# A second PSUM bank for the jobs of a batch, all exponentials of the scan in SBUF, and a new spacing of every job

## The chip, the cores and the metric

The kernel runs on one core of one Trainium2 chip. The metric is the device time in microseconds (us), the median of several executions of the program.

## The reference, cut to what matters

Eight sequences of 512 tokens with 128 channels go through one block: four branches are added to `x`, and then a layer norm and a feed-forward projection follow.

```
xn = layernorm(x) * g + b ;  xp = xn @ w_xproj            # dt_in, B, C (64 states)
delta = softplus(dt_in @ w_dt + b_dt)
h_t = exp(delta_t * A) * h_(t-1) + (delta_t * xn_t) * B_t # 128 channels x 64 states
ssm  = (sum_n h_t * C_t + x * D) @ w_ssm_out
attn = softmax(windowed scores of 16 heads, windows of 32) @ v @ wo
conv = silu(depthwise convolution of x over 4 taps)
mem  = x @ w_wm + 0.3 * softmax(x @ dec.T / sqrt(128)) @ dec   # 512 slots
x1 = x + 0.2 attn + 0.45 ssm + 0.15 conv + 0.2 mem
out = x1 + layernorm(x1) @ W2 + bias                      # W2: int4-rounded weight + low rank
```

## The kernel before, in words

One sequence is a batch, and the kernel's body runs once for each of the 8 batches. The state recurrence sets its beat. It is cut into 64 units. A unit is 2 channels x 64 states on the 128 partitions, 512 steps long, and is one `tensor_tensor_scan` on VectorE. Four units (`q` = 0 to 3) make a group, so a batch has 16 groups. Every engine runs the same loop over the slots `s` = 0 to 63, and what it issues in a slot is written out in its `body`; each engine works in program order and waits on semaphores. Two parities `p` keep the data of one batch apart from those of the next.

What a unit needs:

- ScalarE (`unit_exp`, two slots ahead): the decay `exp(delta * A)` out of `wide`, rows of delta that SyncE's DMA spread over the partitions. For q = 0, 1, 2 it goes to `decay` in SBUF; for q = 3 it goes to the PSUM bank `uP[3]` (line 659).
- The input `delta * xn * B`. For q = 0, 1, 2 TensorE spreads the rows into `uP[q]` (line 905) and VectorE multiplies by `B2` in place (line 1189). For q = 3 the rows come by DMA into `uwide` in SBUF, and GpSimd multiplies them (`pool_input`, line 1407).
- VectorE's scan (line 1201). Of its two inputs one lies in PSUM and one in SBUF, in each of the four cases.
- GpSimd (`pair_product`, line 1391) multiplies the states of two units by C, and TensorE adds them up (`reduce_group`, line 929).

Beside it, in slots of their own, lie the windowed attention of the same batch (scores, line 938; bias and maximum on VectorE, 1214; exponentials on ScalarE, 673; scaling on GpSimd, `prob_norm`, 1396; transposes, 945; values, 953), and the jobs. A job is some matmuls into the PSUM bank `jobP` (bank 7), emptied by ScalarE or VectorE. There are three families, and all share that one bank in the order of `JOB_AT`: "p" prepares the next batch (transposes, dtpre, B, C, q, k, v), "m" is the memory branch (es: scores, pt: transposes of the probabilities) and the convolution of this batch, and "t" ends the batch before (back, zT, ffn). TensorE fills a job only when the job before it in the bank has been emptied (`fill`). ScalarE empties it in the same slot (`EMPTY_LAG` 0). `AT` gives the slots of the other steps: among them `ln_apply`, `scale_xn`, `normalise2`, the softplus chain, `output` (VectorE waits for the ffn job, line 1261), and `gate` (VectorE waits for ScalarE's tanh, line 1236). The projection that gathers the branches (`project`) has 11 steps. In the last batch six of them come before the end of the loop, and the others in `tail`.

Of the kernel before, what the change touches and what calls it, by code (L numbers as in the profile page):

```python
# [12 lines left out]
L = 512  # L13
# [31 lines left out]

JOB_AT = {13: ("t", "back"), 15: ("p", "xaT"), 17: ("p", "xnT"), 19: ("p", "dtpre"),
# [3 lines left out]
EMPTY_LAG = 0  # L50
N_EARLY = 6
JOB_SLOT = {name: s for s, (_, name) in JOB_AT.items()}
# [12 lines left out]
SETUP_AT = 5  # L65


ROWS_AT = {"store": 14, "rows": 15}
VALUE_DMA_AT = {0: (0, 1, 2), 1: (3, 4, 5), 2: (6, 7, 8), 3: (9, 10, 11)}
PART_DMA_AT = {17: 0, 19: 1, 20: 2}  # L70

M_MAX_LAG, M_EXP_LAG, M_INV_LAG, M_DIAG_LAG = 2, 3, 4, 5

SCORES_AT = {33 * k // 10: k for k in range(NBLK)}
BIAS_LAG, EXP_LAG, INV_LAG, NORM_LAG, PT_LAG, PT_COPY_LAG, PV_LAG, AO_COPY_LAG = 2, (3, 4), 6, 5, 9, 9, 11, 11
AHEAD = 2
# [7 lines left out]
def memory_tile_at(s, lag):  # L86

    fam, name = JOB_AT.get(s - lag, ("", ""))
    return int(name[2]) if name[:2] == "es" else None
# [26 lines left out]
def hybrid_block_kernel(nc, x, ln_g, ln_b, w_xproj, w_dt, b_dt, A_log, D_ssm, w_ssm_out, wq, wk, wv,  # L116
# [3 lines left out]
    with ctx:  # L120
# [231 lines left out]
        def _(sp):  # L352
# [142 lines left out]
        def _(act):  # L495
# [132 lines left out]
            def front(B, p):  # L628
# [3 lines left out]
                for name in PRE:  # L632
                    if name == "dtpre":
                        decay_rates()
                    if name == "B":
                        softplus_exp(B)
                        softplus_logs(B)
                    if name == "q":
                        high_parts(B)
                        mid_parts(B)  # L640
                        for part in (1, 2):
                            spread_parts(act, B, p, part)
                        act.wait_ge(const_ready, 3)
                        act.wait_ge(head_tables, 3)
# [48 lines left out]
            def mem_exp(B, t):  # L693
                wait(act, m_max, B * NT + t + 1)
                if t >= 2:
                    wait_job(act, "m", B, f"pt{t - 2}")
                ins = nc.scalar.activation(mprob[:, t % 2, :], jobP[:, :], ACT.Exp, bias=mmx[:, t:t + 1],
                                           accum_out=msum[:, t:t + 1])
# [9 lines left out]
            def memT_copy(B, t):  # L708
                wait_job(act, "m", B, f"pt{t}")
                if t == 0:  # L710
                    wait(act, ready["t"], B * N_TAIL - N_TAIL + 1)
                nc.scalar.activation(mprobT[:, :, t * 128:(t + 1) * 128],
                                     jobP[:, :].rearrange("p (c t) -> p c t", c=4), ACT.Copy).then_inc(done["m"], 1)

            def conv_bias(B):
                wait_job(act, "m", B, "conv")
                wait(act, ready["t"], B * N_TAIL - N_TAIL + 1)
                nc.scalar.activation(cv_v[:, :], jobP[:, :], ACT.Identity, bias=bconv_col).then_inc(cv_step, 1)
                wait(act, cv_step, B * N_CV + CV["v"])
# [26 lines left out]
            def body(B, p):  # L746
                for s in range(UNITS):
# [29 lines left out]
                    if s - EMPTY_LAG in JOB_AT:  # L777
                        empty_job(*JOB_AT[s - EMPTY_LAG], B, p)
                    fam, name = JOB_AT.get(s - 1, ("", ""))
                    if fam == "p" and name in "qk" and not last(B):  # L780
# [27 lines left out]
        def _(pe):  # L808
# [47 lines left out]

            before = [None]

            def fill(fam, B, name):
                if before[0] is not None:  # L860
                    f, b, n = before[0]
                    wait(pe, done[f], job_count(f, b, n))

            def filled(ins, fam, B, name):
                ins.then_inc(ready[fam], 1)
                before[0] = (fam, B, name)

# [89 lines left out]
            def conv_tap(B, p, tap):  # L957
                if tap == 0:
                    fill("m", B, "conv")
                o = HALO - (TAPS - 1) + tap  # L960
                ins = mm(jobP[:, :], convdiag[:, tap, :], xaT[p][:, o:o + L], start=(tap == 0), stop=(tap == TAPS - 1))
                if tap == TAPS - 1:
                    filled(ins, "m", B, "conv")

            def mem_job(name, B, p):
                fill("m", B, name)
                if name[:2] == "es":
                    t = int(name[2])
                    ins = mm(jobP[:, :], xaT[p][:, HALO + t * 128:HALO + (t + 1) * 128], decTs[:, :], start=True,
                             stop=True)  # L970
                else:
                    t = int(name[2])
                    wait(pe, m_diag, B * NT + t + 1)
                    for c in range(4):
                        ins = mm(jobP[:, c * 128:(c + 1) * 128], mprob[:, t % 2, c * 128:(c + 1) * 128],  # L975
                                 mdiag[:, t % 2, :], start=True, stop=True)
# [49 lines left out]
            def body(B, p):  # L1026
                before[0] = ("p", B, "v")
                for s in range(UNITS):
# [30 lines left out]
                    if fam == "p" and not last(B):  # L1059
                        pre_job(name, B + 1, 1 - p)  # L1060
                    if fam == "m" and name != "conv":
                        mem_job(name, B, p)
# [17 lines left out]
        def _(dve):  # L1080
# [391 lines left out]
```

## Time and profile before

| | us |
|---|---|
| median of 3 runs | 1167.07 (1165.49 to 1168.94) |
| profiled execution, its own time | 1166.9 |
| its span, first to last instruction | 1165.1 |
| VectorE (DVE) busy | 988.3 (85%) |
| GpSimd (POOL) busy | 951.5 (82%) |
| TensorE (PE) busy | 866.0 (74%) |
| ScalarE (ACT) busy | 835.1 (72%) |

Busy time is the time in which an engine had at least one instruction under way. Idle time before a group of instructions is put down to what released its first wait. The first scan of batch 0 begins 37.7 us after the start of the span, and the last scan of batch 7 ends at 1141.0 us; the rest is the tail.

### The profile page before, as it was taken

The numbers are of one execution on the slowest core, as the hardware profiler recorded it, in microseconds if no ns is written. First come the engines' busy times: TensorE is split into PE (matmuls) and PEld (weight loads), VectorE is DVE, ScalarE is ACT, GpSimd is POOL, SyncE is SP. The second block draws the span as 40 slices with busy tenths as digits, with TensorE's granted clock in tenths as the row PEclk, the third lists the DMA queues.
The fourth block names the chain that finished last, engine by engine and source line by source line (L and its number), as shares of the span: only waits on it lengthen the run. The fifth ranks groups of instructions, "written<-read, shape, count | busy, mean of one in ns | idle before, by whom it ended". The sixth has DMA issues, their size and how long they took to land. (4 is left out here: it accounts for less than half of the span.)

```text
span 1165.1 us, 19124 instructions
## 1 busy us (share of the span) xinstructions
PE 866.0 (74%) x4151; PEld 361.1 (31%) x4151; DVE 988.3 (85%) x2306; ACT 835.1 (72%) x2247; POOL 951.5 (82%) x668
## 2 busy tenths in 40 slices
PE   4477769687786787777786777867768687778775
PEld 2132323232333233333232333323233233333332
DVE  2699998888897997979989799788998989898992
ACT  4668786877778776777777777587776876766671
POOL 6479997988888887888979898698887988788892
PEclk8558998778897977979889788787989788897797
DMA  5845766565756566566656476555666566656640
GB/s 121 202 127 147 199 164 171 133 169 163 181 153 159 156 158 165 146 155 167 165 166 165 118 192 169 141 147 148 173 167 177 137 166 169 174 157 173 159 113 9
DMA packets 124397, 181.18 MB, mean 156 GB/s; under 512 B 29266, under 2 KB 41062, under 8 KB 124262
## 3 DMA queue, kind: packets, MB, share of 16 engines
q1 hardware_dynamic: 123974, 179.56, 58.9%
q14 instruction: 96, 0.79, 0.3%
q8 instruction: 39, 0.64, 0.2%
q10 hardware_dynamic: 288, 0.20, 0.1%
HBM read 170.79 MB, written 5.05 MB: 151 GB/s over the span
## 5 line engine op out<-in xcount | busy, mean ns | idle before, releaser
L1391 POOL TENSOR_TENSOR prod<-hst,C 128x1024 f32<-128x1024 f32 x256 | 601.7, 2353 | 156.7 <-DVE hst L1201 155.9
L1201 DVE TENSOR_TENSOR_SCAN hst<-decay,bank 128x512 f32<-128x512 f32 x384 | 459.5, 1206 | 16.0 <-POOL prod L1391 15.1
L659 ACT ACTIVATE decay<-wide,A_rep 128x512 f32<-128x512 f32 x384 | 273.9, 715 | 72.8 <-DVE hst L1201 55.0
L1189 DVE TENSOR_TENSOR bank<-bank,B 128x512 f32<-128x512 f32 x384 | 261.7, 681 | 48.8 <-PE bank L938 23.0
L905 PE MATMUL bank<-spread,sel_bc 96*128 96x512 bf16 x384 | 170.0, 444 | 145.3 <-DVE hst L1201 137.0
L673 ACT ACTIVATE prob<-s_sb,nmax 128x96 f32<-128x96 f32 x512 | 184.8, 363 | 1.5 <-DVE nmax L1214 0.5
L1407 POOL TENSOR_TENSOR uwide<-uwide,B 128x512 f32<-128x512 f32 x128 | 162.7, 1271 | 21.8 <-DMA uwide<-u_rows 21.8
L929 PE MATMUL bank<-prod,sel_red 128*32 128x512 f32 x1024 | 171.7, 750 | 2.0 <-POOL prod L1391 2.0
L1201 DVE TENSOR_TENSOR_SCAN hst<-bank,uwide 128x512 f32<-128x512 f32 x128 | 155.0, 1211 | 6.1 <-ACT bank L659 4.6
L938 PE MATMUL bank<-k,q 128*128 128x384 f32 x256 | 133.6, 609 | 7.3 <-DVE nmax L1214 4.8
L945 PE MATMUL bank<-ident,prob 128*96 128x128 f32 x512 | 99.4, 328 | 48.9 <-ACT ao L689 44.2
L905 PEld LDWEIGHTS bank<-spread,sel_bc 96*128 96x128 bf16 x384 | 41.5, 108 | 282.4 <-DVE hst L1201 231.0
L682 ACT ACTIVATE probT<-bank 96x512 f32<-96x512 f32 x128 | 75.1, 587 | 68.4 <-PE bank L945 68.4
L1396 POOL TENSOR_TENSOR prob<-prob,pinv 128x384 f32<-128x384 f32 x128 | 108.9, 851 | 5.7 <-DVE pinv L1222 5.4
L945 PEld LDWEIGHTS bank<-ident,prob 128*96 128x96 f32 x512 | 64.9, 149 | 118.4 <-issue 101.5
L1214 DVE CUSTOM_DVE_ANT_0 s_sb<-bank,bias 128x96 f32<-128x96 f32 x512 | 97.8, 246 | 0.0
L673 ACT ACTIVATION_READ_ACCUMULATOR prob<-s_sb,nmax 128x1 f32 x512 | 96.8, 189 | 0.0
L659 ACT ACTIVATE bank<-wide,A_rep 128x512 f32<-128x512 f32 x128 | 87.0, 680 | 10.8 <-DVE hst L1201 10.8
L689 ACT ACTIVATE ao<-bank 128x128 f32<-128x128 f32 x128 | 33.8, 264 | 64.6 <-PE bank L953 64.6
L938 PEld LDWEIGHTS bank<-k,q 128*128 128x128 f32 x256 | 53.8, 232 | 65.3 <-issue 35.1
L953 PE MATMUL bank<-probT,vw 96*8 96x128 f32 x1024 | 54.2, 285 | 11.2 <-ACT probT L682 11.1
L975 PE MATMUL bank<-mdiag,mprob 128*128 128x128 f32 x256 | 44.0, 326 | 9.5 <-ACT mdiag L706 7.7
(188 smaller groups left out, 1014.6 us busy)
## 6 DMA issues: line engine op xcount, KB each, us to landing
wide<-dt_rows SPq DMA_DIRECT2D x512, 256.0 KB, 4.6
uwide<-u_rows SPq DMA_DIRECT2D x128, 256.0 KB, 4.1
spread<-parts SPq DMA_DIRECT2D x66, 32.0 KB, 3.4
x_sb<-in_L_attn_x_dram SPq DMA_DIRECT2D x8, 256.0 KB, 4.1
dt_rows<-sp_t SPq DMA_DIRECT2D x8, 256.0 KB, 3.9
out_dram<-outb SPq DMA_DIRECT2D x8, 256.0 KB, 2.3
vw<-v_tok SPq DMA_DIRECT2D x80, 16.0 KB, 3.3
u_rows<-uv SPq DMA_DIRECT2D x8, 64.0 KB, 3.6
```

The source lines that it names most:

```text
L659: nc.scalar.activation(to, wide[m % SLOTS][:, s % 2, :], ACT.Exp, scale=A_rep[:, g:g + 1]).then_inc(exp_done, 1)
L673: ins = nc.scalar.activation(prob[:, k % 4, g, :], s_sb[:, k % 2, g, :], ACT.Exp, bias=nmax[:, k % 2, g:g + 1], scale=-1.0, accum_out=psum ...
L905: mm(uP[q][:, :], sel_bc[:, i, :, :].rearrange("k j n -> k (j n)"), spread[p][:, q, :], start=True, stop=True).then_inc(u_ready, 1)
L929: ins = mm(yP[32 * q:32 * q + 32, :], sel_red[:, i, :], prod[:, (i % 2) * 4 + q, :], start=(i == 0), stop=(i == GROUPS - 1), skip_group_ch ...
L938: mm(sP[:, 0:KVH * 3 * W], q4[:, k, :, :].rearrange("p r q -> p (r q)"), k4[:, :, k * W:k * W + 3 * W], start=True, stop=True).then_inc(s_ ...
L945: ins = nc.tensor.transpose(ptP[0:3 * W, g * 128:(g + 1) * 128], prob[:, k % 4, g, :], ident[:, :])
L1189: v.tensor_tensor(uP[s % 4][:, :], uP[s % 4][:, :], B2[p][:, :], ALU.mult).then_inc(dbx_done, 1)
L1201: v.tensor_tensor_scan(hst[:, s % 4, :], kept, into[:, :], 0.0, ALU.mult, ALU.add).then_inc(scan_done, 1)
L1214: ins = v.tensor_tensor_reduce(s_sb[:, k % 2, g, :], sP[:, g * 3 * W:(g + 1) * 3 * W], bias3[:, row, g, :], 1.0, BIG, ALU.add, ALU.min, nm ...
L1391: g.tensor_tensor(prod[:, 2 * (m % 4):2 * (m % 4) + 2, :], hst[:, 2 * (m % 2):2 * (m % 2) + 2, :], C2[p][:, :].unsqueeze(1).to_broadcast([ ...
L1396: g.tensor_tensor(prob[:, k % 4, :, :], prob[:, k % 4, :, :], pinv[:, k % 4, :].unsqueeze(2).to_broadcast([128, KVH, 3 * W]), ALU.mult) \
L1407: g.tensor_tensor(u, u, B2[p][:, :], ALU.mult).then_inc(gbx_done, 1)
```

## The change

The bank `uP[3]` is no longer used by the scan: all four exponentials of a group go to `decay` in SBUF, which grows from 3 to 4 buffers. The bank that this frees, bank 3, becomes `memP` and takes the memory and convolution jobs; `jobP` keeps the other two families, and TensorE remembers for each of the two banks which job it holds. The slots of all jobs and of the steps between them are new, ScalarE empties a job one slot later than it is filled, and of the last batch's projection ten steps lie inside the loop. The job "v" is now third from last of its family, before q and k, and the load of the value windows also waits for the first scores of its batch.

```diff
-PRE = {... ["xaT", "xnT", "dtpre", "B", "C", "q", "k", "v"]}
-MEM = {... ["es0", "pt0", "conv", "es1", "es2", "pt1", "es3", "pt2", "pt3"]}
+PRE = {... ["xaT", "xnT", "dtpre", "B", "C", "v", "q", "k"]}
+MEM = {... ["es0", "es1", "pt0", "es2", "pt1", "es3", "pt2", "conv", "pt3"]}
-JOB_AT = {13: ("t", "back"), 15: ("p", "xaT"), 17: ("p", "xnT"), 19: ("p", "dtpre"),
-          22: ("t", "zT"), 26: ("t", "ffn"), 28: ("m", "es0"), 32: ("p", "B"), 33: ("p", "C"), 34: ("m", "pt0"),
-          39: ("m", "conv"), 42: ("m", "es1"), 46: ("m", "es2"), 50: ("m", "pt1"), 51: ("m", "es3"),
-          55: ("m", "pt2"), 57: ("m", "pt3"), 58: ("p", "q"), 60: ("p", "k"), 62: ("p", "v")}
-EMPTY_LAG = 0
-N_EARLY = 6
+JOB_AT = {14: ("t", "back"), 18: ("p", "xaT"), 20: ("p", "xnT"), 22: ("p", "dtpre"), 24: ("t", "zT"),
+          28: ("t", "ffn"), 33: ("p", "B"), 35: ("p", "C"), 37: ("p", "v"), 52: ("p", "q"), 56: ("p", "k")}
+MEM_AT = {10: "es0", 15: "es1", 19: "pt0", 22: "es2", 27: "pt1", 31: "es3", 36: "pt2", 41: "conv", 47: "pt3"}
+EMPTY_LAG = 1
+LAST_PROJECT = {48: (0,), 50: (1,), 53: (2,), 54: (3,), 55: (4,), 56: (5,), 62: (6, 7), 63: (8, 9)}
 AT = {
-    "reduce": 3, "y_copy": 5, "project": 1, "proj_copy": 12, "residual": 14, "aggr2": 16, "root2": 17,
-    "normalise2": 20, "ffn": 25, "output": 27,
-    "ln_stats": 0, "ln_aggr": 2, "ln_root": 4, "ln_apply": 11, "scale_xn": 12, "softplus_exp": 20,
-    "softplus_logs": 21, "rounding": 23, "log1p": 24, "dt": 25, "u": 27, "high": 30, "r": 32,
-    "mid": 35, "lo": 37,
-    "tanh": 39, "gate": 40,
+    "reduce": 3, "y_copy": 5, "project": 1, "proj_copy": 13, "residual": 16, "aggr2": 18, "root2": 19,
+    "normalise2": 22, "ffn": 27, "output": 31,
+    "ln_stats": 0, "ln_aggr": 2, "ln_root": 4, "ln_apply": 13, "scale_xn": 15, "softplus_exp": 24,
+    "softplus_logs": 25, "rounding": 27, "log1p": 28, "dt": 29, "u": 30, "high": 32, "r": 34,
+    "mid": 36, "lo": 38,
+    "tanh": 42, "gate": 44,
 }
-M_MAX_LAG, M_EXP_LAG, M_INV_LAG, M_DIAG_LAG = 2, 3, 4, 5
+M_MAX_LAG, M_EXP_LAG, M_INV_LAG, M_DIAG_LAG = 2, 3, 5, 6
-BIAS_LAG, ..., PT_LAG, PT_COPY_LAG, PV_LAG, AO_COPY_LAG = 2, (3, 4), 6, 5, 9, 9, 11, 11
+BIAS_LAG, ..., PT_LAG, PT_COPY_LAG, PV_LAG, AO_COPY_LAG = 2, (3, 4), 6, 5, 9, 9, 10, 11
...
-        uP, yP, sP, ptP, jobP = bank[0:4], bank[4], bank[5], bank[6], bank[7]
+        uP, memP, yP, sP, ptP, jobP = bank[0:POOL_Q], bank[3], bank[4], bank[5], bank[6], bank[7]
-        decay = sb("decay", [128, POOL_Q, L])
+        decay = sb("decay", [128, 4, L])
...
 def window_values(B, which):
     wait(sp, done["p"], job_count("p", B, "v"))
+    wait(sp, s_ready, B * NBLK + 1)
...
 def unit_exp(B, s):
-    to = uP[q][:, :] if q == POOL_Q else decay[:, q, :]
-    nc.scalar.activation(to, wide[m % SLOTS][:, s % 2, :], ACT.Exp,
+    nc.scalar.activation(decay[:, q, :], wide[m % SLOTS][:, s % 2, :], ACT.Exp,
                          scale=A_rep[:, g:g + 1]).then_inc(exp_done, 1)
...
 def unit_scan(B, s):
     if q == POOL_Q:
-        kept, into = uP[q][:, :], uwide[(i // 2) % U_SLOTS][:, i % 2, :]
+        into = uwide[(i // 2) % U_SLOTS][:, i % 2, :]
     else:
-        kept, into = decay[:, q, :], uP[q]
+        into = uP[q]
-    v.tensor_tensor_scan(hst[:, s % 4, :], kept, into[:, :], 0.0, ALU.mult, ALU.add)
+    v.tensor_tensor_scan(hst[:, s % 4, :], decay[:, s % 4, :], into[:, :], 0.0, ALU.mult, ALU.add)
...
 # mem_job, conv_tap, mem_max, mem_exp, memT_copy, conv_bias, conv_gate: memP in place of jobP
-before = [None]
+before = {"job": None, "mem": None}        # fill() and filled() take the entry of the job's bank
...
-    if last(B) and 0 < s - JOB_SLOT["pt3"] <= N_EARLY:
-        project(B, p, s - JOB_SLOT["pt3"] - 1)
+    if last(B):
+        for n in LAST_PROJECT.get(s, ()):
+            project(B, p, n)
 def tail(B, p):
-    for n in range(N_EARLY, N_PROJ - 1):
-        project(B, p, n)
     reduce_group(B, GROUPS - 1)
```

## Rows read from the trace of the kernel before

**Rows 1.** Page, part 1: busy us, share of the span, instructions of each engine.

```profile
PE 866.0 (74%) x4151; PEld 361.1 (31%) x4151; DVE 988.3 (85%) x2306; ACT 835.1 (72%) x2247; POOL 951.5 (82%) x668
```

**Rows 2.** Windows: length, then busy us of each engine; batches 1 and 6, tail.

```profile
175.70:314.00 138.30, 108.14 (x515) 44.66 (x515) 121.29 (x285) 103.20 (x280) 117.80 (x82) 0.82 0.62 160
...
872.80:1010.40 137.60, 105.08 (x517) 44.92 (x517) 121.66 (x285) 103.11 (x280) 117.70 (x82) 0.85 0.61 161
...
1141.00:1165.10 24.10, 12.43 (x42) 5.64 (x38) 2.65 (x11) 3.53 (x7) 4.13 (x6) 0.72 0.04 11
```

**Rows 3.** Windows of batch 2's groups 0 to 15: length, PE, PEld, DVE, ACT, POOL.

```profile
314.00:325.10 11.10, 11.10 (x40) 4.71 (x41) 8.81 (x25) 5.83 (x16) 7.33 (x5) 0.78 0.79 200
325.10:332.20 7.10, 6.51 (x23) 2.21 (x22) 7.10 (x17) 4.81 (x13) 5.51 (x5) 1.00 0.53 144
332.20:341.60 9.40, 7.92 (x39) 3.17 (x37) 7.88 (x27) 6.27 (x18) 9.09 (x11) 1.00 0.60 164
341.60:350.40 8.80, 6.31 (x37) 3.25 (x41) 8.60 (x23) 7.61 (x23) 8.80 (x7) 0.81 0.49 131
350.40:357.70 7.30, 5.46 (x39) 2.09 (x39) 7.30 (x22) 5.79 (x20) 6.33 (x4) 1.00 0.80 202
357.70:368.50 10.80, 5.91 (x25) 2.49 (x21) 8.16 (x18) 10.38 (x24) 9.50 (x10) 0.68 0.40 108
368.50:381.50 13.00, 9.94 (x44) 4.67 (x45) 7.92 (x18) 7.47 (x24) 9.14 (x6) 0.61 0.71 182
381.50:389.80 8.30, 6.48 (x35) 2.62 (x35) 8.30 (x26) 7.92 (x24) 7.92 (x5) 1.00 0.20 65
389.80:397.00 7.20, 6.41 (x37) 2.96 (x37) 7.20 (x20) 5.84 (x15) 7.10 (x5) 1.00 0.74 205
397.00:404.00 7.00, 6.40 (x32) 2.21 (x31) 6.98 (x16) 4.96 (x19) 7.00 (x5) 1.00 0.97 227
404.00:413.70 9.70, 5.64 (x23) 2.27 (x24) 7.92 (x18) 6.88 (x21) 7.39 (x6) 0.69 0.65 162
413.70:421.80 8.10, 6.51 (x46) 2.13 (x46) 7.82 (x19) 5.73 (x18) 7.88 (x6) 0.95 0.55 157
421.80:430.20 8.40, 6.71 (x32) 2.85 (x32) 8.40 (x28) 6.00 (x18) 6.91 (x5) 0.68 0.79 188
430.20:438.40 8.20, 6.57 (x34) 2.84 (x31) 7.30 (x13) 5.70 (x17) 6.64 (x5) 0.71 0.43 130
438.40:444.60 6.20, 5.14 (x42) 2.94 (x40) 6.20 (x9) 5.17 (x11) 5.96 (x5) 1.00 0.73 185
444.60:451.20 6.60, 2.55 (x20) 0.61 (x12) 5.76 (x7) 6.11 (x12) 6.26 (x4) 0.81 0.54 148
```

**Rows 4.** Timeline, 364.5 to 368.6 us: start, duration; two POOL rows, then DVE.

```profile
364.92 1.28 POOL L1407 TENSOR_TENSOR uwide<-uwide,B 128x512 f32<-128x512 f32 x1
366.15 1.29 POOL L1396 TENSOR_TENSOR prob<-prob,pinv 128x384 f32<-128x384 f32 x1
...
365.86 0.89 DVE L1168 SCALAR_TENSOR_TENSOR sp_t<-sp_t,xn 128x512 f32<-128x512 f32 x1 [1.96 <-ACT sp_l L616]
```

**Rows 5.** One line's durations, min/median/max in ns; and a group, mean ns.

```profile
L1396 POOL TENSOR_TENSOR prob<-prob,pinv x128: 815/826/1287, 57.4 to 1128.2; 128x384 f32<-128x384 f32 x128
...
L1201 DVE TENSOR_TENSOR_SCAN hst<-bank,uwide 128x512 f32<-128x512 f32 x128 | 155.0, 1211 | 6.1 <-ACT bank L659 4.6 <-POOL uwide L1407 1.5
```

**Rows 6.** Groups on DVE: busy us, mean ns, idle before and its releaser.

```profile
L1261 DVE TENSOR_TENSOR outb<-bank,x 128x512 f32<-128x512 f32 x8 | 5.5, 691 | 37.9 <-PE bank L1002 37.9
L1236 DVE SCALAR_TENSOR_TENSOR cs<-bank,cols,cv_a 128x512 f32<-128x512 f32 x8 | 6.0, 751 | 15.3 <-ACT cv_a L723 15.3
```

**Rows 7.** A group on ACT, the memory branch's exponential: busy us, mean ns.

```profile
L697 ACT ACTIVATE mprob<-bank,mmx 128x512 f32<-128x512 f32 x32 | 21.5, 671 | 0.0
```

**Rows 8.** Timeline of the tail, 1141 to 1147 us: POOL's last product, then PE.

```profile
1141.17 2.35 POOL L1391 TENSOR_TENSOR prod<-hst,C 128x1024 f32<-128x1024 f32 x1
...
1145.45 1.07 PE L929 MATMUL bank<-prod,sel_red 128*32 128x512 f32 x8
```

More of the change, by code:

```diff
@@ new lines @@
+MEM_AT = {10: "es0", 15: "es1", 19: "pt0", 22: "es2", 27: "pt1", 31: "es3", 36: "pt2", 41: "conv", 47: "pt3"}
+EMPTY_LAG = 1
+LAST_PROJECT = {48: (0,), 50: (1,), 53: (2,), 54: (3,), 55: (4,), 56: (5,), 62: (6, 7), 63: (8, 9)}
+MEM_SLOT = {name: s for s, name in MEM_AT.items()}
+AT = {
+    "reduce": 3, "y_copy": 5, "project": 1, "proj_copy": 13, "residual": 16, "aggr2": 18, "root2": 19,
[4 more added lines that the diff above has]
+    "tanh": 42, "gate": 44,
@@ L86, in memory_tile_at @@
 def memory_tile_at(s, lag):
-    fam, name = JOB_AT.get(s - lag, ("", ""))
+    name = MEM_AT.get(s - lag, "")
     return int(name[2]) if name[:2] == "es" else None
@@ L637, in front @@
                         softplus_logs(B)
-                    if name == "q":
+                    if name == "v":
                         high_parts(B)
@@ L642, in front @@
                             spread_parts(act, B, p, part)
+                    if name == "q":
                         act.wait_ge(const_ready, 3)
@@ L696, in mem_exp @@
                     wait_job(act, "m", B, f"pt{t - 2}")
-                ins = nc.scalar.activation(mprob[:, t % 2, :], jobP[:, :], ACT.Exp, bias=mmx[:, t:t + 1],
+                ins = nc.scalar.activation(mprob[:, t % 2, :], memP[:, :], ACT.Exp, bias=mmx[:, t:t + 1],
                                            accum_out=msum[:, t:t + 1])
@@ L717, in conv_bias @@
                 wait(act, ready["t"], B * N_TAIL - N_TAIL + 1)
-                nc.scalar.activation(cv_v[:, :], jobP[:, :], ACT.Identity, bias=bconv_col).then_inc(cv_step, 1)
+                nc.scalar.activation(cv_v[:, :], memP[:, :], ACT.Identity, bias=bconv_col).then_inc(cv_step, 1)
                 wait(act, cv_step, B * N_CV + CV["v"])
@@ L778, in body @@
                         empty_job(*JOB_AT[s - EMPTY_LAG], B, p)
-                    fam, name = JOB_AT.get(s - 1, ("", ""))
+                    if s - EMPTY_LAG in MEM_AT:
+                        empty_job("m", MEM_AT[s - EMPTY_LAG], B, p)
+                    fam, name = JOB_AT.get(s - EMPTY_LAG - 1, ("", ""))
                     if fam == "p" and name in "qk" and not last(B):
@@ L854, in setup_step @@
                     pe.wait_ge(w_scaled, 4)
-            before = [None]
+            before = {"job": None, "mem": None}
             def fill(fam, B, name):
-                if before[0] is not None:
-                    f, b, n = before[0]
+                held = before["mem" if fam == "m" else "job"]
+                if held is not None:
+                    f, b, n = held
                     wait(pe, done[f], job_count(f, b, n))
@@ L865, in filled @@
                 ins.then_inc(ready[fam], 1)
-                before[0] = (fam, B, name)
+                before["mem" if fam == "m" else "job"] = (fam, B, name)
             def pre_job(name, B, p, front=False):
@@ L960, in conv_tap @@
                 o = HALO - (TAPS - 1) + tap
-                ins = mm(jobP[:, :], convdiag[:, tap, :], xaT[p][:, o:o + L], start=(tap == 0), stop=(tap == TAPS - 1))
+                ins = mm(memP[:, :], convdiag[:, tap, :], xaT[p][:, o:o + L], start=(tap == 0), stop=(tap == TAPS - 1))
                 if tap == TAPS - 1:
@@ L965, in mem_job @@
             def mem_job(name, B, p):
+                if name == "es0":
+                    wait(pe, done["m"], B * N_MEM)
                 fill("m", B, name)
@@ L968, in mem_job @@
                     t = int(name[2])
-                    ins = mm(jobP[:, :], xaT[p][:, HALO + t * 128:HALO + (t + 1) * 128], decTs[:, :], start=True,
+                    ins = mm(memP[:, :], xaT[p][:, HALO + t * 128:HALO + (t + 1) * 128], decTs[:, :], start=True,
                              stop=True)
@@ L1026, in body @@
             def body(B, p):
-                before[0] = ("p", B, "v")
+                before["job"], before["mem"] = ("p", B, "k"), None
                 for s in range(UNITS):
@@ L1060, in body @@
                         pre_job(name, B + 1, 1 - p)
-                    if fam == "m" and name != "conv":
-                        mem_job(name, B, p)
-                    if last(B) and 0 < s - JOB_SLOT["pt3"] <= N_EARLY:
-                        project(B, p, s - JOB_SLOT["pt3"] - 1)
+                    if s in MEM_AT and MEM_AT[s] != "conv":
+                        mem_job(MEM_AT[s], B, p)
+                    if last(B):
+                        for n in LAST_PROJECT.get(s, ()):
+                            project(B, p, n)
             def tail(B, p):
-                for n in range(N_EARLY, N_PROJ - 1):
-                    project(B, p, n)
                 reduce_group(B, GROUPS - 1)
@@ L1235, in conv_gate @@
                 wait(dve, ready["t"], B * N_TAIL - N_TAIL + 1)
-                v.scalar_tensor_tensor(cs[:, :], jobP[:, :], bconv_col, cv_a[:, :], ALU.add, ALU.mult).then_inc(cv_step, 1)
+                v.scalar_tensor_tensor(cs[:, :], memP[:, :], bconv_col, cv_a[:, :], ALU.add, ALU.mult).then_inc(cv_step, 1)
                 wait(dve, cv_step, B * N_CV + CV["cs"])
```

21 lines of the change are left out of this document (10 added, 11 removed).

## The prediction

> **What bounds the kernel now.** I first read the busy shares. VectorE has 988.3 us and GpSimd 951.5 us of a span of 1165.1 [rows 1]: two engines are within 200 us of the span, and neither fills it. Then the stretches by batch: batches 1 and 6 take 138.3 and 137.6 us from last scan to last scan [rows 2], and from 175.7 to 1010.4 us six batches take 139.1 each. In one, VectorE works 121.3 and GpSimd 117.8 us. So a batch leaves VectorE about 18 us of idle time and GpSimd 21. Then the groups of one batch [rows 3]. Groups 3, 4, 7, 8, 9, 12 and 14 are as long as VectorE's busy time in them or at most 0.2 us longer, and 3, 8 and 9 are GpSimd's as well (8.80 of 8.80, 7.10 of 7.20, 7.00 of 7.00). The idle time of VectorE lies in a few groups: 0 (2.3 us), 2 (1.5), 5 (2.6; ScalarE is busy for 10.38 of 10.80), 6 (5.1) and 10 (1.8). Two causes have a name and a price: `output` waits 37.9 us for TensorE and the gate 15.3 us for ScalarE [rows 6]. The kernel is bound by VectorE and GpSimd together where nothing disturbs them, and by late jobs elsewhere.
>
> **The change, part by part.**
>
> *The exponential of q = 3 in SBUF.* This is the part that costs. The scan of q = 3 reads `uwide` in SBUF and, until now, its decay in PSUM. Afterwards both inputs are in SBUF. What that does is in the trace, at the only VectorE instruction of the loop that reads two SBUF tensors beside a busy GpSimd, the rounding step of line 1168 [rows 4]. GpSimd's L1407 runs from 364.92 to 366.20. The rounding step starts at 365.86 and ends at 366.75, 0.55 us after GpSimd's instruction. The next GpSimd instruction, L1396, starts at 366.15 and takes 1.29 us, where its median is 0.826 [rows 5]. So VectorE waited until GpSimd's instruction was through, and then GpSimd waited for VectorE. The seven occurrences in the loop show the same; none runs beside GpSimd undisturbed. The Trainium skill says it as a rule, in "SBUF — State Buffer", section "SBUF: two separate sides": VectorE with two SBUF inputs and a GpSimd instruction that reads SBUF share one pair of ports under an exclusive lock, the first to start has it for its whole instruction, and the other waits. The trace agrees (0.55 us behind GpSimd's end, and 0.46 us taken from GpSimd). No row shows the scan itself with two SBUF inputs.
>
> The price of one such scan to GpSimd: the rounding step needed the ports for 0.55 us and took 0.46 from GpSimd, 0.09 less. A form like it with one input in PSUM takes 0.75 [rows 6], so 0.20 of an instruction lies outside the ports' time. The scan takes 1.21 [rows 5]: 1.21 - 0.20 - 0.09 = 0.92 us. The bounds are 0 (no lock for this form) and 1.21. I take 0.92. The price to VectorE is what is left of GpSimd's instruction: 0 to 2.35 us (a product, [rows 8]). The mean GpSimd instruction is 951.5 / 668 = 1.42 us; half of it, by the busy share 0.82, is 0.58. If all were products it would be 0.96. I take 0.58.
>
> There are 16 such scans in a batch, one in each group. A group's new length is the largest of its old length, VectorE's time + 0.58, and GpSimd's time + 0.92. On the rows of [rows 3] this adds: group 1 0.58, group 2 0.61, group 3 0.92, group 4 0.58, group 7 0.58, group 8 0.82, group 9 0.92, group 11 0.70, group 12 0.58, group 14 0.68, group 15 0.58, and nothing in 0, 5, 6, 10 and 13, whose idle time hides it. Sum: 7.55 us per batch. The wait for the ports stands in front of everything that VectorE has queued: the next unit's multiplication, the bias steps, and with them GpSimd's next product. By the rule's words, a whole instruction of 1.21 for GpSimd, the same table gives 9.8 us per batch and a time of 1217; that is within my range.
>
> The writing ScalarE I charge nothing. An exponential of this size from PSUM into SBUF takes 0.67 us [rows 7]; even 0.1 us more for each of 16 would be 1.6 us on an engine that idles for some 35 us of a batch [rows 2], and a gain as small is as possible.
>
> *Two banks and new slots: what they save.* `output` moves from one slot behind the ffn job to three behind it. The wait was 37.9 us with the tail's 9.6 in it, which stays: 28.3 over seven batches, 4.0 each, all in group 6. What is late next there is GpSimd (9.14 + 0.92 = 10.06), so of 13.0 us no more than 2.9 can go. I take 2.9. The gate moves from one slot behind the convolution's bias to two; of group 10's 9.7 us, VectorE's 7.92 + 0.58 = 8.5 stay, so 1.2 go. The bounds for each are 0 and that. At the start of a batch, job v (slot 62) and the memory jobs (to slot 57) no longer stand on TensorE next to the projection; group 0 has 11.1 us against 8.81 + 0.58. The projection's order is unchanged, and TensorE is busy for all 11.1. I take 0.5 of 1.7. Together 4.6 us per batch. That jobs wait less for their bank is in these numbers; no wait of VectorE besides them names it. The softplus rounding keeps its two slots behind the logarithms, and I leave its wait.
>
> *What they cost.* Three of the four memory exponentials and the first transposed copy now lie in slots 13 to 25, about groups 3 to 6, where none lay: 4 x 0.67 = 2.7 us at the size of [rows 7]. It is ScalarE's densest stretch: 7.61 + 5.79 + 10.38 + 7.47 = 31.25 us of 39.9, and the stretch would shrink by the 2.9 above. Bounds 0 and 2.7; I take half, 1.3.
>
> *Small moves, at nothing.* ScalarE empties a job a slot later; jobs of one bank are now at least two slots apart, and the slot between, about 2 us, hides it; without it TensorE would wait for the copy, at most the 0.67 us of [rows 7]. The u rows are stored at slot 32, and are wanted from slot 56: 24 slots cover that. The last part of u is spread by DMA at slot 42 and wanted at 62. On SyncE the value windows now wait for the first scores of their batch, and behind them stand `wide` loads: those are four pairs, or 8 units, ahead, some 17 us; the values are wanted from slot 10. Without that cover a slip of 1 to 2 us would show at `unit_exp`. Values a slot earlier: ScalarE's copy before it is in the same order.
>
> *Tail.* Projection steps 6 to 9 leave it. TensorE's last reduction starts at 1145.45 though GpSimd's product was through at 1141.17 + 2.35 = 1143.52 [rows 8]: 1.9 us go.
>
> **Sum.** Per batch 7.55 - 4.6 + 1.3 = 4.25 us, by 8 batches 34.0. Span 1165.1 + 34.0 - 1.9 = 1197.2. The profiled execution took 1166.9, 1.8 more than its span: **1199 us**. It lies 0.2 below the median of the three runs, so the same holds for that.
>
> **The rivals.**
>
> *A, the scan is not held up.* The form is another than line 1168's. For it: no row shows it. Against: all seven rows of the loop with two SBUF inputs show the wait, and nothing in them depends on the arithmetic. Then (-4.6 + 1.3) x 8 - 1.9 = -28: 1139 us, faster.
>
> *B, the wait is there, and the new slots even out the groups.* The wait then decides only through GpSimd's total: 118 + 16 x 0.92 = 132.7 us per batch, and 16 x 0.58 + 121.3 = 130.6 for VectorE. A batch is 139.1 now. If the new slots leave 4 us of idle time instead of 21, a batch is 137: 8 x -2.1 - 1.9 gives 1148, faster. It decides where GpSimd's idle time falls below 139.1 - 132.7 = 6.4 us per batch. Against it: groups 0 and 6 alone have 7.6 us of GpSimd idle time now, and slots 28, 29 and 30 now carry three GpSimd steps in a row.
>
> *C, both prices add up.* VectorE waits, so GpSimd's product comes late, so the next scan of q = 3 meets it in the middle. The eleven groups that I charged then pay 0.58 + 0.92 = 1.5 each: 16.5 - 3.3 = 13.2 per batch, 1165.1 + 105.6 - 1.9 + 1.8 = 1271 us.
>
> *D, gains and price cancel.* Within 0.3%, 1164 to 1171; it needs a wait at half its price.
>
> **How the numbers follow.** Forecast 0.61, with its own range 1172 to 1240; A 0.12, B 0.11, C 0.11, D 0.05. What a measurement of this kernel can tell from no change is 0.3%, 3.5 us. Faster is A and B, 0.23; within it is D, 0.05; slower is the forecast and C, 0.72. The range 1140 to 1245 takes in B, D and the forecast; most of A and C lie outside.
>
> **What would show it.** Right: scans of line 1201 with `uwide` longer than 1.21 us on the mean (about 1.8), the scans of q = 0 to 2 unchanged; GpSimd's L1407 or L1391 longer in one case per group, by some 0.9 us, and GpSimd's busy time about 118 us up; the wait before L1261 down to the tail's 9.6, that before L1236 near nothing; batches of about 143 us; the last reduction 1.9 us sooner after the last scan. Wrong: `uwide` scans still at 1.21 us (A), or groups 3, 8 and 9 no longer than before (B), or batches over 150 us (C). If ScalarE is idle in groups 3 to 6 as now, the 1.3 was wrong.

## The result: 2.25% slower, and the profile after

The changed kernel takes 1193.86 us at the median of 4 runs (1189.67 to 1196.35), the kernel before 1167.24 (4 runs). The ratio is 1.0225, with a 95% interval of 1.0189 to 1.0260. The forecast was 1199 us and slower.

The page of the changed kernel, part 1 (busy us, share of the span, instructions), beside [rows 1]:

```profile
PE 868.0 (73%) x4151; PEld 344.3 (29%) x4151; DVE 1070.8 (90%) x2306; ACT 840.2 (70%) x2247; POOL 1050.9 (88%) x668
```

The same instructions are there in the same number, and the span grew by 29.5 us (1165.1 to 1194.6). But VectorE is busy for 82.5 us more and GpSimd for 99.4 us more. The costliest groups of its page say where. Their columns are busy us, mean ns, idle before and its releaser; the lines moved by a few (1201 is now 1206, 1407 is 1412, 1391 is 1396, 1396 is 1401).

```profile
L1396 POOL TENSOR_TENSOR prod<-hst,C 128x1024 f32<-128x1024 f32 x256 | 601.6, 2353 | 87.6 <-DVE hst L1206 85.5
L1206 DVE TENSOR_TENSOR_SCAN hst<-decay,bank 128x512 f32<-128x512 f32 x384 | 458.0, 1203 | 35.9 <-POOL prod L1396 28.2
...
L1412 POOL TENSOR_TENSOR uwide<-uwide,B 128x512 f32<-128x512 f32 x128 | 246.5, 1926 | 22.7 <-DMA uwide<-u_rows 22.7
L1206 DVE TENSOR_TENSOR_SCAN hst<-decay,uwide 128x512 f32<-128x512 f32 x128 | 241.0, 1883 | 1.4 <-POOL uwide L1412 1.4
...
L1401 POOL TENSOR_TENSOR prob<-prob,pinv 128x384 f32<-128x384 f32 x128 | 119.3, 932 | 3.0 <-DVE pinv L1227 2.0
```

Compare the third and the fourth line with the second and with [rows 5]. The scans of q = 0 to 2 take 1203 ns. Those of q = 3, which had taken 1211, take 1883: 128 x 0.672 = 86 us. GpSimd's L1412, which often follows such a scan, has a mean of 1926 ns; it took 1.28 us in [rows 4], where nothing held it. 128 x (1.926 - 1.271) = 84 us, with the kernel before's mean of 1271 ns. The products themselves are unchanged at 2353.

The timeline of the changed kernel (start, duration), one row of VectorE and then three of GpSimd, shows one such meeting:

```profile
354.61 2.96 DVE L1206 TENSOR_TENSOR_SCAN hst<-decay,uwide 128x512 f32<-128x512 f32 x1
...
354.15 2.35 POOL L1396 TENSOR_TENSOR prod<-hst,C 128x1024 f32<-128x1024 f32 x1
356.45 2.19 POOL L1412 TENSOR_TENSOR uwide<-uwide,B 128x512 f32<-128x512 f32 x1
358.61 2.34 POOL L1396 TENSOR_TENSOR prod<-hst,C 128x1024 f32<-128x1024 f32 x1
```

The product runs from 354.15 to 356.50. The scan starts at 354.61 and ends at 357.57, 1.07 us after the product. L1412 has started at 356.45, but takes 2.19 us instead of 1.27: 0.92 us more, the figure of the prediction. The distance from its start to the next one's says the same: 2.16 us here, 1.23 in [rows 4]. The waits do not appear as idle time; they lie inside the durations. That is why both engines look busier, and why the column of idle time does not show them.

It is not one meeting alone. The list of this line's durations (min/median/max in ns) has the rest:

```profile
L1206 DVE TENSOR_TENSOR_SCAN hst<-decay,uwide x128: 1200/1852/3274, 47.0 to 1167.9; 128x512 f32<-128x512 f32 x128
```

The shortest is as fast as before, so two inputs in SBUF do not slow the scan by themselves. In the trace 25 of the 128 take 1.20 to 1.22 us. Each of the other 103 met a GpSimd instruction that was under way when it started, and ended 1.08 us after it. On GpSimd 112 instructions, most of them L1412, are longer than undisturbed, most by 0.92 us.

The windows of batch 2, groups 0, 2, 4 to 10, answer to [rows 3] (length, then PE, PEld, DVE, ACT, POOL):

```profile
328.90:338.50 9.60, 7.74 (x27) 2.90 (x25) 9.60 (x25) 4.43 (x12) 6.96 (x4) 1.00 0.71 175
...
346.20:357.60 11.40, 8.45 (x32) 2.69 (x30) 9.60 (x26) 4.86 (x14) 11.09 (x12) 0.85 0.73 187
...
366.40:376.80 10.40, 7.90 (x51) 3.94 (x49) 10.25 (x28) 9.59 (x32) 7.62 (x5) 0.84 0.75 191
376.80:384.90 8.10, 5.14 (x30) 1.97 (x29) 8.10 (x18) 5.77 (x15) 7.87 (x8) 1.00 0.28 82
384.90:396.00 11.10, 8.35 (x44) 4.26 (x43) 8.49 (x20) 10.70 (x23) 8.50 (x6) 0.85 0.56 143
396.00:406.50 10.50, 8.57 (x37) 3.66 (x37) 9.06 (x28) 9.03 (x30) 10.20 (x7) 0.67 0.36 101
406.50:414.20 7.70, 5.53 (x26) 1.96 (x26) 7.70 (x20) 4.76 (x14) 7.69 (x5) 0.78 0.84 219
414.20:422.80 8.60, 7.44 (x46) 3.72 (x45) 7.57 (x17) 7.96 (x25) 8.60 (x6) 1.00 0.78 192
422.80:431.50 8.70, 6.99 (x42) 2.79 (x40) 7.69 (x18) 6.97 (x21) 8.70 (x6) 1.00 0.70 175
```

Groups 8 and 9 went from 7.2 and 7.0 to 7.7 and 8.6 us, and GpSimd fills them. Group 2 grew from 9.4 to 11.4. Group 0 fell from 11.1 to 9.6, group 6 from 13.0 to 11.1 and group 10 from 9.7 to 8.7. The moved slots also shifted time between groups: 4 and 7 grew by 3.1 and 2.2, and 5 fell by 2.7.

By stretches of the span, from last scan to last scan (worked out from the scans' rows of each profile; mean of batches 1 to 6):

| us | first scan | batch 0 | batches 1 to 6, each | batch 7 | tail |
|---|---|---|---|---|---|
| before | 37.7 | 137.9 | 139.1 | 130.7 | 24.1 |
| after | 37.5 | 150.1 | 141.8 | 131.7 | 24.4 |
| e1, SBUF exponential alone | 37.4 | 146.3 | 144.6 | 136.8 | 22.1 |
| e2, after without the second SBUF input | 37.5 | 140.7 | 130.8 | 120.0 | 22.2 |
| e5, before with later output and gate | 38.3 | 141.2 | 141.5 | 129.7 | 25.8 |
| e7, after with the memory jobs later | 38.1 | 144.6 | 140.5 | 129.9 | 23.0 |
| e9, three banks in turn, memory later | 38.1 | 142.8 | 135.0 | 129.0 | 24.2 |

### The profile page after: what moved, and what is told of

It reads as the page before. It is cut to its first block and busy times, and to the rows that moved or that the text cites. A ratio compares the mean times of both kernels' runs of the same rounds, so it can differ in the third digit from the quotient of the medians.

```text
span 1194.6 us, 19156 instructions
## 1 busy us (share of the span) xinstructions
PE 868.0 (73%) x4151; PEld 344.3 (29%) x4151; DVE 1070.8 (90%) x2306; ACT 840.2 (70%) x2247; POOL 1050.9 (88%) x668
## 5 line engine op out<-in xcount | busy, mean ns | idle before, releaser
L1206 DVE TENSOR_TENSOR_SCAN hst<-decay,bank 128x512 f32<-128x512 f32 x384 | 458.0, 1203 | 35.9 <-POOL prod L1396 28.2
L659 ACT ACTIVATE decay<-wide,A_rep 128x512 f32<-128x512 f32 x512 | 363.5, 715 | 118.0 <-DVE hst L1206 105.4
L909 PE MATMUL bank<-spread,sel_bc 96*128 96x512 bf16 x384 | 172.4, 453 | 168.0 <-DVE hst L1206 157.5
L1412 POOL TENSOR_TENSOR uwide<-uwide,B 128x512 f32<-128x512 f32 x128 | 246.5, 1926 | 22.7 <-DMA uwide<-u_rows 22.7
L1206 DVE TENSOR_TENSOR_SCAN hst<-decay,uwide 128x512 f32<-128x512 f32 x128 | 241.0, 1883 | 1.4 <-POOL uwide L1412 1.4
L942 PE MATMUL bank<-k,q 128*128 128x384 f32 x256 | 129.5, 593 | 4.3 <-ACT k L568 3.2
L1401 POOL TENSOR_TENSOR prob<-prob,pinv 128x384 f32<-128x384 f32 x128 | 119.3, 932 | 3.0 <-DVE pinv L1227 2.0
L957 PE MATMUL bank<-probT,vw 96*8 96x128 f32 x1024 | 57.3, 300 | 31.7 <-ACT probT L682 15.6
L689 ACT ACTIVATE ao<-bank 128x128 f32<-128x128 f32 x128 | 33.5, 262 | 37.5 <-PE bank L1003 31.3
L957 PEld LDWEIGHTS bank<-probT,vw 96*8 96x8 f32 x1024 | 16.6, 88 | 119.2 <-ACT probT L682 57.5
L975 PE MATMUL bank<-decTs,xaT 128*128 128x512 f32 x64 | 43.8, 773 | 0.0
```

What stands on the lines that cost most here:

```text
L659: nc.scalar.activation(decay[:, q, :], wide[m % SLOTS][:, s % 2, :], ACT.Exp, scale=A_rep[:, g:g + 1]).then_inc(exp_done, 1)
L909: mm(uP[q][:, :], sel_bc[:, i, :, :].rearrange("k j n -> k (j n)"), spread[p][:, q, :], start=True, stop=True).then_inc(u_ready, 1)
L942: mm(sP[:, 0:KVH * 3 * W], q4[:, k, :, :].rearrange("p r q -> p (r q)"), k4[:, :, k * W:k * W + 3 * W], start=True, stop=True).then_inc(s_ ...
L1206: v.tensor_tensor_scan(hst[:, s % 4, :], decay[:, s % 4, :], into[:, :], 0.0, ALU.mult, ALU.add).then_inc(scan_done, 1)
L1401: g.tensor_tensor(prob[:, k % 4, :, :], prob[:, k % 4, :, :], pinv[:, k % 4, :].unsqueeze(2).to_broadcast([128, KVH, 3 * W]), ALU.mult) \
L1412: g.tensor_tensor(u, u, B2[p][:, :], ALU.mult).then_inc(gbx_done, 1)
```

## The experiments

The theory (M, for meeting) was the prediction's: the scan with two SBUF inputs and GpSimd wait for each other, the new slots give some of it back, the second bank by itself gives nothing. The main rival (S, for slots) was that these waits are hidden and that the new slots made the kernel slower.

**e1, one part of the change alone.** The kernel before, with this:

```diff
-    to = uP[q][:, :] if q == POOL_Q else decay[:, q, :]
+    to = decay[:, q, :]
-    kept, into = uP[q][:, :], uwide[...]
+    kept, into = decay[:, q, :], uwide[...]
```

> The kernel before with one part of the change alone: the q = 3 exponential goes to a fourth decay buffer in SBUF; one job bank, old slots. Theory M (the scan with two SBUF inputs and GpSimd's instructions wait for each other): the table of the prediction adds 7.55 us per batch, so 1167 + 60 = 1227 us (1205 to 1245); uwide scans at 1.6 to 1.9 us, GpSimd's L1407 at about 1.9 us. Rival S (the ports' waits are hidden, the new slots are what made the change slower): 1165 to 1180 us, with the scans longer but the batches not.

Measured: 1211.69 us, ratio 1.0368 (1.0351 to 1.0386), 44 us above the kernel before. S falls. The price is real, and three quarters of the 60 us of M's table: the change adds 5.5 us to a batch, where the table had 7.55. By groups (means of batches 1 to 6, from the scans' rows) the table was less good than by its sum. Groups 0, 1, 4 and 12 came out 2.9 us below it, groups 2 and 5 came out 2.5 above it, and the others together 1.7 below. Group 2 grew by 2.0 us, more than both prices of one scan together.

**e2, the change without the meeting.** The changed kernel, with a second input from PSUM; the input of the q = 3 channels is left out, while GpSimd still does its work on it.

```diff
-    into = uwide[(i // 2) % U_SLOTS][:, i % 2, :]
+    into = uP[2]          # and unit_u for q = 2 waits for that scan too
```

> The changed kernel, but the q = 3 scan takes its second input from the PSUM bank uP[2] in place of uwide; it leaves out the input of the q = 3 channels, and GpSimd still computes it. No scan has two SBUF inputs. Theory M: the whole port price goes, 1194 - 55 = about 1139 us (1125 to 1155), uwide products on GpSimd back to 1.27 us. Rival S: 1180 to 1195 us, since slots and banks are as in the changed kernel.

Measured: 1105.76 us, ratio 0.9465 (0.9439 to 0.9491). Its page has, on GpSimd and on VectorE:

```profile
L1412 POOL TENSOR_TENSOR uwide<-uwide,B 128x512 f32<-128x512 f32 x128 | 162.9, 1273 | 22.8 <-DMA uwide<-u_rows 22.8
...
L1206 DVE TENSOR_TENSOR_SCAN hst<-decay,bank 128x512 f32<-128x512 f32 x512 | 611.8, 1205 | 26.1 <-POOL prod L1396 18.0 <-PE bank L942 5.7 <-POOL uwide L1412 1.6
```

All 512 scans are back at 1.2 us and L1412 at 1.27. Same slots, same banks, same GpSimd work, and 88 us less than the changed kernel. ScalarE still writes all exponentials to SBUF here, so the price does not come from these writes. It is 88 us in the new slots, twice what it is in the old ones. Whatever TensorE's clock gave is in these 88 us: the granted clock was 0.87 in this run and 0.83 in the changed kernel, and no run separates the two. For e1's 44 us this doubt does not arise, at 0.82 against 0.83 in the kernel before. The same run shows what the new slots with two banks are worth together: 62 us below the kernel before. M's 1139 was 33 us too high, and its range ended at 1125, since it took the price from the old slots' table.

**e10, half the dose.** e2 in the odd groups, the changed kernel in the even ones; the input of the odd groups' q = 3 channels is left out.

```diff
-    into = uP[2]
+    into = uwide[(i // 2) % U_SLOTS][:, i % 2, :] if i % 2 == 0 else uP[2]
```

> e2 for the odd groups, the changed kernel for the even ones: half of the q = 3 scans (64) read two SBUF inputs; the odd groups' q = 3 input is left out. Theory M says the price is paid by each scan: midway between 1106 and 1194, 1150 us (1140 to 1160). If the price were hidden until GpSimd is full, it would lie nearer to 1106: below 1130 us.

Measured: 1155.38 us, against 1150 for midway. From e2, 64 such scans cost 50 us; from there to the changed kernel the other 64 cost 38.5. So in the new slots the price is paid from the first scans on, and not only once GpSimd is full.

**e4 and e4b, the second bank alone.** The changed kernel's banks and exponentials, with all slots, lags and orders of the kernel before.

```diff
-JOB_AT, MEM_AT, AT, ..., EMPTY_LAG = 1         # the new slots
+JOB_AT, MEM_AT, AT, ..., EMPTY_LAG = 0         # the slots of before, m jobs still in memP
```

> Both banks and all exponentials in SBUF, but every slot and lag as before. Against e1 it shows the second bank alone. Theory M: no wait of VectorE named the bank, so it is within 0.5% of e1 (about 1227 us). Rival K (waiting for the one bank holds up TensorE and what stands behind it): 10 to 20 us below e1.

> As e4, with ScalarE's wait for GpSimd's tables back in its old place (in e4 it stood in front of the first job, and the first scan began 9.3 us later). Theory M: the second bank alone is worth nothing at the old slots, so 1212 us, within 0.3% of e1. Rival: 1 to 2% off e1 in either direction.

Measured: e4 1220.79 us, with its first scan at 46.7 us in place of 37.4, for the reason that the second text gives; e4b 1212.37, against 1211.69 for e1. In the old slots the second bank by itself is worth nothing. No run has the new slots with one bank, so how the 62 us of e2 divide between bank and slots stays open.

**e5, two waits moved, with one bank.** The kernel before, with the waits for `output` and the gate moved out of the way. One projection step of the last batch also goes to the tail (`N_EARLY` 5), and the tail grew by 1.7 us.

```diff
-..., 28: es0, 32: B, 33: C, 34: pt0, 39: conv, 42: es1, 46: es2, 50: pt1, 51: es3, 55: pt2, 57: pt3, 58: q, 60: k, 62: v
+..., 30: es0, 34: B, 35: C, 36: pt0, 40: conv, 43: es1, 47: es2, 51: pt1, 52: es3, 56: pt2, 58: pt3, 59: q, 61: k, 63: v
-"output": 27, "tanh": 39, "gate": 40
+"output": 29, "tanh": 40, "gate": 42
```

> The kernel before (one bank, q = 3 exponential in PSUM) with output two slots later, gate one slot further from the convolution, and the jobs behind them moved by one or two slots. It asks how much of the new slots' gain is these two waits. Theory M: 4.0 + 1.9 us per batch go where nothing else is late, 7 x 5.5 = 38 us: 1129 us. Rival: ScalarE (busy 10.4 of 10.8 us in group 5) or GpSimd is late next, and less than half comes: above 1148 us.

Measured: 1185.50 us, ratio 1.0152 (1.0104 to 1.0201): slower than before. M missed by 56 us. The rival's "above 1148" holds, but neither side expected a loss. A line of VectorE in its trace:

```profile
L1189 DVE TENSOR_TENSOR bank<-bank,B 128x512 f32<-128x512 f32 x384 | 262.6, 684 | 96.3 <-PE bank L938 74.8 <-PE bank L905 15.5 <-issue 4.7
```

The wait for the gate is gone, that for `output` is down to the tail's 9.6 us, and group 6 fell to 11.1 us. But VectorE now waits 74.8 us for scores on TensorE (23.0 before). A possible reason is that in one bank the late jobs stand closer together at a batch's end, and a TensorE that waits for the bank holds up the scores queued behind it; no run took these apart. What the run does show: with one bank, moving these jobs by a slot or two does not bring the gain. The bank is worth nothing in the old slots (e4b), and these moved slots, which are not the new ones, cost 18 us with one bank.

**e7, the memory jobs out of ScalarE's dense stretch.** The changed kernel, with

```diff
-MEM_AT = {10: "es0", 15: "es1", 19: "pt0", 22: "es2", 27: "pt1", 31: "es3", 36: "pt2", 41: "conv", 47: "pt3"}
+MEM_AT = {26: "es0", 30: "es1", 34: "pt0", 37: "es2", 41: "pt1", 44: "es3", 47: "pt2", 51: "conv", 55: "pt3"}
```

> The changed kernel with the memory and convolution jobs in slots 26 to 55 in place of 10 to 47, out of ScalarE's dense stretch (the last batch's projection moves behind them). Theory M: groups 3 to 6 get shorter by about 1.3 us per batch, 10 us in all: 1184 us. Rival: it is VectorE's and GpSimd's waits for each other that fill these groups too, and moving the work costs as much later: within 0.5% of 1192.

Measured: 1181.92 us, 12 below the changed kernel, as M said. Batches 1 to 6 fell by 1.3 us each, which is the term of the sum; batch 0 fell by 5.5. The 1.3 is a net figure. Groups 3 to 6 got shorter by 2.3 us together and groups 7 and 10 by 1.7, while 8 and 9 grew by 2.4 (means of batches 1 to 6), so it is in part luck that the term was met to the digit.

**e3, the value windows.** TensorE waits 21.2 us for them in the changed kernel, seven times up to 3.8 us; the kernel before has 1.3 us on this line. The wait list of the changed kernel:

```profile
PEld bank L957 <- DMA vw<-v_tok: 21.2, 7, 3.8
```

```diff
-VALUE_DMA_AT = {0: (0, 1, 2), 1: (3, 4, 5), 2: (6, 7, 8), 3: (9, 10, 11)}
+VALUE_DMA_AT = {0: (0, 1, 2), 1: (3, 4, 5, 6), 2: (7, 8, 9, 10, 11)}
```

> The changed kernel with the last value-window loads issued at pair 1 and 2 of the batch, not behind SyncE's wait at pair 3. Theory V: TensorE's 21.2 us of waits for vw (3.0 in each of seven batches, in group 2) end, group 2 falls from 11.4 to about 10 us, and the time by 7 x 1.4 = 10 us to about 1184. Rival: the wait is hidden behind GpSimd's 11.1 us of work in that group; within 0.3% of 1194.

Measured: 1191.42 us, 0.2% below the changed kernel, less than can be told apart, as the rival said. The wait is gone from the list, and group 2 stayed at 11.4 us, so it was off the path.

**e6, e8, e9 and e11, toward a version that beats both.** The wish is e2's time with all of the computation: two job banks, and the q = 3 decay in PSUM. Three banks then have to carry four units.

```diff
-    unit s uses uP[q], and q = 3 uses decay[3]
+    unit s uses uP[s % 3], units 0 to 62; unit 63 uses decay[3]
-    wait(scan_done, B * UNITS + s - 3)
+    wait(scan_done, B * UNITS + s - 2)        # where a bank is asked for, s >= 3
```

> The changed kernel with all its slots and both job banks, but the three banks uP go in turn over units 0 to 62, whatever q is, so that the q = 3 decay lies in PSUM again; each bank is asked for one unit sooner than with four. Only unit 63 keeps two SBUF inputs: 8 such scans in place of 128. Theory M: the price of the ports goes and e2's time comes with the whole computation, 1106 to 1120 us. Rival R: with three banks TensorE and ScalarE get a bank one scan later (about 1.9 us), VectorE then waits for them: 1150 us or more.

Measured: 1184.80 us, ratio 1.0142. M's 1106 to 1120 missed, and R's "1150 or more" holds. The port price is gone (120 of the 128 scans at 1.21 us), and most of it came back as waits: ScalarE before the q = 3 exponential, VectorE for scores behind TensorE's wait for a bank.

```profile
ACT bank L660 <- DVE hst L1208: 131.4, 44, 6.3
...
DVE bank L1195 <- PE bank L943: 82.1, 50, 4.2
```

e8 only reorders the queues:

```diff
+    if s % 4 == POOL_Q - 1: unit_exp(B, s + 1)        # q = 3: one slot later than the others
-    unit_u(B, p, s + AHEAD)                           # first in TensorE's slot
+    unit_u(B, p, s + AHEAD)                           # last in TensorE's slot
```

> As e6 (three banks in turn, one scan per batch with two SBUF inputs), but what waits for a bank no longer stands in front of other work: ScalarE issues the q = 3 exponential one slot later, and TensorE spreads a unit's rows at the end of its slot. Theory R (e6 lost to waits in the queues: ScalarE 131 us before the q = 3 exponential, VectorE 82 us for scores queued on TensorE behind a unit): both shrink, and the time goes toward e2's 1106: 1110 to 1140 us, faster than before. Rival: three banks are too few whatever the order; 1165 us or more.

Measured: 1167.64 us (10 runs, 1157.86 to 1178.81), ratio 0.9996 (0.9966 to 1.0026): 17 us below e6, and not faster than the kernel before. The expectation of 1110 to 1140 missed. ScalarE's wait fell from 131.4 to 72.9 us. VectorE's 82 us for scores went, and 80 us of waits for the spread rows (line 913) stand in their place. Either the bank comes free too late, or the spread, now last in TensorE's slot, is itself too late; in e6, where it came first, these waits were 21.5 us. No run took the two apart.

e9 adds e7's slots.

> e8 with the memory and convolution slots of e7. If ScalarE's dense stretch costs the same without the ports' waits, 8 to 12 us below e8; if e7 gained only because the waits made ScalarE late, within 0.5% of e8.

Measured: 1145.56 us, ratio 0.9817 (0.9773 to 0.9861), 22 us below e8. That is more than either side expected, and more than the 12 of e7. A possible reason is that ScalarE's dense stretch costs more where the waits for the ports do not hide it; no run shows it by itself. Its page:

```profile
PE 843.6 (74%) x4151; PEld 340.5 (30%) x4151; DVE 1000.6 (87%) x2306; ACT 833.9 (73%) x2247; POOL 957.4 (84%) x668
```

GpSimd is back at 957 us (951.5 before) and VectorE at 1001 (988.3).

e11 is e9 with e3's edit.

> e9 with the last value-window loads issued at pair 1 and 2, as in e3. In e3 the end of TensorE's wait for them gave next to nothing, with GpSimd busy for all of group 2. Theory: without the ports' waits GpSimd still has 9.2 of 9.5 us there, so again next to nothing, within 0.5% of e9's 1145.6. Rival: TensorE's 23 us of waits were on the path now, 10 to 20 us less: 1126 to 1136 us.

Measured: 1145.37 us over 5 rounds, ratio 0.9814 (0.9796 to 0.9831): the same as e9, and 1.9% faster than the kernel before. e9 and e11 compute the whole of the reference. They are still 40 us above e2. The largest wait that VectorE has more than in e2 is for TensorE's spread rows, 64.6 us in e9 against 11.6. It fits the bank that comes a unit later as well as the spread that e8 put last; no run took it away.

## Why the prediction was right, point by point

- *The mechanism and the sign*: right, shown by e1 (the part alone), e2 (the part taken away) and e10 (half of it).
- *0.92 us per scan for GpSimd, 0.58 for VectorE*: the first is what most of the meetings took, but not every scan had one. GpSimd's busy time rose by 99.4 us where the prediction had 118, with 112 of its instructions longer and not 128. The second was 0.67 on the mean (1883 - 1211).
- *The table, 7.55 us per batch*: 5.5 in the old slots (e1), with errors of both signs in its rows. It was too high there, and far too low in the new ones, where e2 against the changed kernel gives 11.0. The table charged the price to the old groups and then took the gain off. But an idle time can be used once: the slots either close it up or it hides the waits. The four means of batches 1 to 6 show it: 139.1 and 144.6 in the old slots without and with the price, 130.8 and 141.8 in the new ones.
- *The gain of the slots, 4.6 us per batch*: 139.1 - 130.8 = 8.3 without the price (e2 against before; ScalarE's dense stretch is in it), and 144.6 - 141.8 = 2.8 with it (e1 against after). The named waits went as forecast: the rows below, of the changed kernel, have 9.6 us before L1266 (37.9 in [rows 6]) and none before L1241 (15.3). But the named waits were only part of what the new slots could close: group 0, where a gain of 0.5 was taken, fell by 1.5 in batch 2.
- *ScalarE's dense stretch, 1.3*: e7 gives 1.3 for batches 1 to 6, as a net of larger gains and losses.
- *Per batch 4.25*: measured 2.7. *All batches alike*: wrong. Batch 0 grew by 12.2 us. It has no `output` wait that could be saved and pays the price (8.4 in e1). It also has memory jobs in the slots of the one-time setup, and was 5.5 us shorter where e7 moved them. 6 x 2.7 + 12.2 + 1.0 + 0.3 - 0.2 = 29.5, the whole difference of the spans. Against the sum, batches 1 to 6 came out 9.3 us lower, batch 0 8.0 higher, batch 7 3.2 lower and the tail 2.2 higher: the span was forecast at 1197.2 and is 1194.6. The sign and the mechanism were not luck. That the number came this close was in part luck: the forecast was 1.55 us too long for each of six batches and 8 us too short for batch 0.
- *The value windows "at nothing"*: the time was right, the reason wrong. I looked at the loads behind the new wait, not at the last of the four value loads. That one stands behind SyncE's wait for a scan at pair 3, and the values were moved a slot toward it.
- *Tail -1.9 us*: the reduction did start sooner, 2.5 us after the last scan in place of 4.4. In e2, with the same slots, the tail was indeed 1.9 shorter (22.2). But e1 has 22.1 with the old slots: its last scan waits for GpSimd and ends later, the projection is through 2.1 us after it, and the reduction starts 2.5 us after it all the same. So the move of the steps was not needed for this gain. In the changed kernel the tail is 0.3 longer than before, as the last section shows.
- *Two readings of the rows*: GpSimd's busy time is 214 us below the span and not "within 200". Group 1, which VectorE fills as well (7.10 of 7.10), is missing from the list of full groups. The sum uses neither.

```profile
L1241 DVE SCALAR_TENSOR_TENSOR cs<-bank,cols,cv_a 128x512 f32<-128x512 f32 x8 | 5.9, 740 | 0.0
L1266 DVE TENSOR_TENSOR outb<-bank,x 128x512 f32<-128x512 f32 x8 | 5.5, 686 | 9.6 <-PE bank L1008 9.6
```

The rivals: A (the scan is not held up) falls by its premise, and its size was too small besides, since without the meeting the slots and the bank give 62 us, not 28. B (the slots even out the groups, faster) fails. Its sign, groups 3, 8 and 9 no longer than before, came only for group 3, which stayed at 8.8 us. GpSimd still idles 10.9 us of batch 2's 141.1, where B needed less than 6.4. C (both prices add in every full group, 1271 us) fails as a whole, and group 2 shows it in one place. D (no change) falls with the result.

## What to carry to other kernels

Before a tensor is moved from PSUM to SBUF to free a bank, look at which instruction then reads two SBUF tensors beside a busy GpSimd: one such scan in four cost 44 us here in loose slots and 88 us in tight ones. These waits lie inside the durations and not in the idle time, so compare mean durations of the same form. And do not subtract a gain and add a price that both live on the same idle time: work out the new schedule without the price first, and then ask what is left to hide it.

## What the runs showed of the hardware that was not expected

In the changed kernel's profile the tail's gain was given back while TensorE's clock was low. The rows are TensorE's in the tail of the changed kernel (start, duration, idle before), and then the windows around them (length, PE busy, granted clock):

```profile
1172.63 1.93 PE L933 MATMUL bank<-prod,sel_red 128*32 128x512 f32 x8 [3.00 <-POOL prod L1396]
1175.28 2.08 PE L1003 MATMUL bank<-yT,w_ssm 128*128 128x512 f32 x2 [0.72 <-ACT yT L665]
```

```profile
1170.20:1172.60 2.40, 0.00 (x0) 0.84 0.00 0
1172.60:1177.40 4.80, 4.01 (x10) 0.50 0.00 0
```

With projection steps 6 to 9 moved into the loop, TensorE had nothing to do for 3.0 us before the last reduction. Then the granted clock was 0.50, the 1.2 GHz level. The reduction took 1.93 us in place of the 1.07 of [rows 8], and the projection step behind it 2.08 in place of 1.12. The same stretches of the kernel before, where the projection kept TensorE busy up to the reduction, are at 1.00:

```profile
1141.00:1145.40 4.40, 4.40 (x14) 1.00 0.00 0
1145.40:1148.40 3.00, 2.24 (x11) 1.00 0.00 0
```

Idle time does not bring the low clock every time. In e2, with the same projection slots, 2.38 us of it stood before the last reduction, and the clock stayed at 1.00:

```profile
1083.20:1085.50 2.30, 0.01 (x1) 1.00 0.00 0
1085.50:1089.30 3.80, 2.19 (x10) 1.00 0.00 0
...
1085.59 1.06 PE L933 MATMUL bank<-prod,sel_red 128*32 128x512 f32 x8 [2.38 <-POOL prod L1396]
```

No run varied this idle time alone, so its part in the fall of the clock is not shown by an experiment.

The second was the order in which the two engines get their turn. In the timeline above GpSimd's next instruction was ready when the product ended, yet the scan that had waited since 354.61 went first and cost GpSimd 0.92 us. None of the 103 scans that had to wait let a second GpSimd instruction pass: each ended 1.08 us after the one that it had met. That L1412's recorded start, 356.45, lies before the product's end says nothing about the order, since GpSimd's instructions overlap in the record by some 0.04 us wherever they follow each other without a pause, also in the kernel before ([rows 4]).
